# Moving a normalization step by one slot, widening a PSUM-slot rule, shifting two weight chunks, and transposing a row through HBM in a two-layer transformer kernel

## The chip, the cores and the metric

The kernel runs on all 8 cores of one Trainium2 chip. Each core computes one of the 8 sequences of the batch on its own; no data goes between cores. The metric is the device time of the slowest core, in microseconds.

## What is computed

Two "sandwich" layers, `x = x + LN(f(LN(x)))` each time, on x of 2048 x 1024 per core:

```python
# layer 0: latent attention, causal, 16 heads, head size 64 + 32 rotary
scores = einsum('bhqd,bhkd->bhqk', Q, K); scores = clip(scores, -80, 80); causal mask
attn = softmax(scores / sqrt(96)) @ V ; out = attn @ W_O
# layer 0: FFN with 8-bit fixed-point inputs and weights, ReLU, 1024 -> 4096 -> 1024
# layer 1: plain attention, not causal, 16 heads of 64
# layer 1: FFN with ternary weights and RMS norm of both inputs
def _ternary_linear(x, w):
    alpha = mean(abs(w)); w_t = sign(w) * (abs(w) > 0.5 * alpha)
    rms = sqrt(sum(x * x, -1)) / sqrt(d)
    return einsum('bsd,fd->bsf', x / (rms + EPS), w_t)
h = gelu(_ternary_linear(x, w_up)); out = _ternary_linear(h, w_down)
```

## The kernel before

**The program.** Each engine has its own list of instructions, in the order in which the Python code calls `P.op` and `P.group`. Waits are worked out from named resources: a reader waits for the last writer, a writer for the last writer and all readers. An engine runs its list strictly in order, so a wait at its head holds all behind it, DMA issues too. DMAs are issued from SP (`sync`), from ACT (`scalar`) and from POOL (`gpsimd`). A DMA waits as its resources say, and also for the DMA four places earlier on its own queue.

**An attention head** (`emit_attention_head`, used by both layers). Keys are in 16 blocks of 128, queries in two halves of 1024. An item n is one key block against one half: `emit_scores` (two matmuls of 512 columns, L462), `emit_expmask` (one Exp on ACT from PSUM to `pbuf`, L481; in layer 0 also a clamp and a mask on DVE, L485 and L492) and `emit_pv` (two matmuls that accumulate into `psB`, L512). The causal layer has 8 items in the first half (n = 0 to 7) and 16 in the second (8 to 23), layer 1 has 16 and 16 (0 to 15, 16 to 31). After the items come "extras", projections for the next head (8 in layer 0; 4 in layer 1, in every second head). Step n of the loop emits: the exp of item n-1, the scores of item n, the PV of item n-2, then `norm_tick(n)`. `pbuf` has two slots, item n uses slot n % 2, so the exp of n waits for the PV of n-2.

The scores go to one of three PSUM slots, by `slot_of(n)`: `psA.s0`, `psA.s1`, and as third the half of `psB` that PV is not accumulating into (banks b0 and b1 while the second half runs). Just after the first half is done, b0 and b1 still hold its result, so the items in a window at the start of the second half are "unsafe" and take `n % 2` in `psA` instead of the third slot.

**Normalizing a head.** When the last PV of the first half is emitted, blocks 0 and 1 are queued. Each `norm_tick` first emits a due "s2", then an "s1" of the next queued block. s1 is a reciprocal of the 1 x 512 row of sums on DVE (L525) and a copy of the block to `scrA` (ACT L531 in layer 0, DVE L535 in layer 1). s2 is a matmul with one row that broadcasts the reciprocal back into the block's PSUM bank (L544) and a multiply on DVE that reads this bank (L551 in even heads, L557 in odd ones). For layer 1, s1(0) is emitted at n = 18, s1(1) at 19, s2(0) at 20, s2(1) at 21. For layer 0 the four are at n = 10, 11, 12 and 13. Blocks 2 and 3 follow likewise after the last item; where there are no extras they are emitted at the end, outside the loop.

**The mean of |w|** (`mk_alpha`). 128 chunks of the two ternary weights are loaded on ACT's queue (L1515) through a ring of two and summed by an ACT Abs (L1501). `chunk()` number i emits the Abs of chunk i-2, then the load of chunk i, so 130 calls do it all. 32 calls lie in the V projection of layer 1, 12 at the start of each of its 8 head pairs, and `emit_block_ffn1` emits what is left (two calls) before it uses the sums (L1552).

**The last FFN** (`emit_block_ffn1`, `emit_ffn_matmul_phase`). It runs over 4 groups of 512 tokens (jt). Each has an up phase (8 weight bands `w1b`, L1028, with a sum of squares by a ones-matmul into `ps_dn0`, L1647), then `down_pre`, then a down phase (16 weight chunks `w2b` in two buffers, L1051), then the closing layer norm. In jt = 0 the weights come in f32 from SP and POOL (L975, L1004), are quantized on DVE (L1083, L1086) and stored from ACT; in jt = 1 to 3 the quantized bands and chunks are loaded from POOL (L964, L993). `down_pre` turns the 512 sums of squares, one row, into a factor per token (scale L1664, square root on ACT L1667, add L1669, reciprocal L1672) and turns the row into four columns of `rstd2T`. The columns are used only as `scale` in the closing layer norm (L368), after the whole down phase. The POOL DMAs of chunks 0 and 1 are emitted behind `down_pre`.

Of the kernel before, what the change touches and what calls it, by code (L numbers as in the profile page):

```python
# [10 lines left out]
F32 = mybir.dt.float32  # L11
# [414 lines left out]
def emit_attention_head(P, h, qk_lhsT, qk_rhs, qk_res, v_km, attn, psA, psB,  # L426
# [4 lines left out]
    half_last = {}  # L431
# [7 lines left out]
    N = len(items)  # L439
# [3 lines left out]
    def slot_of(n):  # L443
        s = n % 3
        half = items[n][1] if n < N else 1
        unsafe = (n < N and half == 1 and n < half_last[0] + 7)
        if s == 2 and unsafe:
            s = n % 2
        if s < 2:
            return psA, s * 1024, (f"psA.s{s}",)  # L450
        w = (1 - half) * 1024
        return psB, w, (f"psB.b{2 * (1 - half)}", f"psB.b{2 * (1 - half) + 1}")
# [86 lines left out]
    def emit_norm_s2(b):  # L539
        bres = f"psB.b{b}"  # L540
        rr = rrow[b % 2]
        scr = scrA[b % 2]
        sres = f"scrA{b % 2}"
        P.op("tensor", lambda e, b=b, rr=rr: e.matmul(  # L544
            psB[0:64, b * 512:(b + 1) * 512], P.consts["ones_f"][0:1, 0:64],
            rr[:], start=True, stop=True),
            reads=(f"rrow{b % 2}", "c_ones_f", sres), writes=(bres,))
        col0 = (h // 2) * S + b * 512
        if not odd:
            P.op("vector", lambda e, scr=scr, col0=col0, b=b:  # L550
                 e.tensor_tensor(attn[0:64, col0:col0 + 512],  # L551
                                 scr[:], psB[0:64, b * 512:(b + 1) * 512],
                                 ALU.mult),
                 reads=(sres, bres), writes=("attn",))
        else:
            P.op("vector", lambda e, scr=scr, b=b:
                 e.tensor_tensor(astage[:, b * 512:(b + 1) * 512],  # L557
                                 scr[:], psB[0:64, b * 512:(b + 1) * 512],
                                 ALU.mult),
                 reads=(sres, bres), writes=("astage",))  # L560

    norm_s1q = []
    norm_s2q = []

    def norm_tick(n):
        if norm_s2q and norm_s2q[0][0] <= n:
            emit_norm_s2(norm_s2q.pop(0)[1])
        if norm_s1q:
            b = norm_s1q.pop(0)
            emit_norm_s1(b)  # L570
            norm_s2q.append((n + 2, b))

    for n in range(M + 2):
        if 1 <= n < M + 1:
# [23 lines left out]
    if odd:  # L598
        col0 = (h // 2) * S
        P.op("gpsimd", lambda e, col0=col0: e.dma_start(  # L600
            out=attn[64:128, col0:col0 + S], in_=astage[:]),
            reads=("astage",), writes=("attn",), dma=True)
# [636 lines left out]
def emit_block_l1(P, hw):  # L1239
# [8 lines left out]
        writes=("v_km.ones",))  # L1248
# [19 lines left out]
    else:  # L1268
# [20 lines left out]
        out=vwT[:].rearrange("p (k m) -> p k m", m=D),  # L1289
        in_=vwt_h.rearrange("(k p) m -> p k m", p=128)),  # L1290
        writes=("vwT",), dma=True)
    for kc in range(NT):
        fns = []
        for dc in range(NCH):
            for n2 in range(2):
# [4 lines left out]
                    start=(dc == 0), stop=(dc == 7)))  # L1300
# [6 lines left out]
            reads=("psA.s0", "v_km.ones", "VBC"), writes=("v_km",))  # L1307
# [114 lines left out]
    for j in range(8):  # L1422
        bs = j % 2
        qpair, kpair = qpair_b[bs], kpair_b[bs]
        qpr, kpr = f"qpair{bs}", f"kpair{bs}"
        if "alpha" in hw:
            for _ in range(12):
                hw["alpha"]["chunk"]()
        if j + 1 < 8:
            pair_loads(j + 1)  # L1430
        for hh in range(2):
            h = 2 * j + hh
            base = hh * 64

            def qk_lhsT(kc, base=base, kpair=kpair):
                return kpair[base:base + 64, kc * 128:(kc + 1) * 128]

            def qk_rhs(lo, width, base=base, qpair=qpair):
                return qpair[base:base + 64, lo:lo + width]

            extra = pair_prod_items(j + 1) if (hh == 0 and j + 1 < 8) else ()
            emit_attention_head(
                P, h, qk_lhsT, qk_rhs, (qpr, kpr), v_km, attn,
                psA, psB, pbuf, causal=False, exp_scale=1.0,
                exp_bias=negb[bs][:], exp_bias_res=f"negb{bs}",
                clamp=None, mask0=None, scrA=scrA, rrow=rrow, astage=astage,
                extra_items=extra, evac_eng="vector")
            if hh == 0 and j + 1 < 8:
                pair_bounds(j + 1)
# [8 lines left out]
        out=owT[:].rearrange("p (k m) -> p k m", m=D),  # L1458
        in_=owt_h.rearrange("(k p) m -> p k m", p=128)),
        writes=("owT",), dma=True)  # L1460
# [5 lines left out]
    for i in range(NT):  # L1466
        half = i % 2
        pres = f"psA.s{half}"
        fns = []
        for c in range(NCH):  # L1470
            for n2 in range(2):
# [4 lines left out]
                    start=(c == 0), stop=(c == 7)))  # L1476
# [55 lines left out]
def emit_block_ffn1(P, hw):  # L1532
# [4 lines left out]
                                kind="Internal").ap()  # L1537
    wdnq_hbm = P.nc.dram_tensor("wdnq_scr", [DFF, D], BF16,
                                kind="Internal").ap()

    al = hw["alpha"]
    while al["idx"][0] < 130:
# [48 lines left out]
    else:  # L1591
# [6 lines left out]
         reads=("lnd.var",), writes=("lnd.sv",))  # L1598
    P.op("vector", lambda e: e.tensor_tensor(
        sv[:], sv[:], stats["rstd"][:], ALU.mult),  # L1600
        reads=("lnd.sv", "lnd.rstd"), writes=("lnd.rms",))
    P.op("vector", lambda e: e.tensor_scalar(
        sv[:], sv[:], float(EPS_RMS), None, ALU.add),
        reads=("lnd.rms",), writes=("lnd.d2",))
    P.op("vector", lambda e: e.reciprocal(scl[:], sv[:]),
         reads=("lnd.d2",), writes=("lnd.f",))
    P.op("vector", lambda e: e.tensor_tensor(
        scl[:], stats["rstd"][:], scl[:], ALU.mult),
        reads=("lnd.f", "lnd.rstd"), writes=("lnd.scl",))
    P.op("vector", lambda e: e.tensor_tensor(  # L1610
        nms[:], stats["mean"][:], scl[:], ALU.mult),
        reads=("lnd.scl", "lnd.mean"), writes=("lnd.nms",))
    P.op("vector", lambda e: e.tensor_scalar(
        nms[:], nms[:], -1.0, None, ALU.mult),
        reads=("lnd.nms",), writes=("lnd.nms",))
# [16 lines left out]
    r2row = P.sb("r2row", [1, 512], F32, st_mm)  # L1632
    rstd2T = P.sb("rstd2T", [128, 4], F32, st_mm)
# [7 lines left out]
    phase = {}  # L1641
# [19 lines left out]
    def down_pre(jt, _ps=[None]):  # L1661
        rms_mm(31)
        ps_dn0 = phase["ps_dn0"]
        P.op("vector", lambda e: e.tensor_scalar(  # L1664
            r2row[:], ps_dn0[:, 0:512][0:1, :], float(1.0 / DFF), None,
            ALU.mult), reads=("ps_dn0",), writes=("r2row",))
        P.op("scalar", lambda e: e.activation(  # L1667
            r2row[:], r2row[:], AF.Sqrt), reads=("r2row",), writes=("r2row",))
        P.op("vector", lambda e: e.tensor_scalar(  # L1669
            r2row[:], r2row[:], float(EPS_RMS), None, ALU.add),  # L1670
            reads=("r2row",), writes=("r2row",))
        P.op("vector", lambda e: e.reciprocal(r2row[:], r2row[:]),  # L1672
             reads=("r2row",), writes=("r2row",))
        for qc in range(4):
            P.op("tensor", lambda e, qc=qc: e.matmul(
                phase["ps_dn1"][:, 0:1], r2row[0:1, qc * 128:(qc + 1) * 128],
                P.consts["ones_f"][0:1, 0:1], start=True, stop=True),
                reads=("r2row", "c_ones_f"), writes=("ps_dn1",))
            P.op("vector", lambda e, qc=qc: e.tensor_copy(
                rstd2T[:, qc:qc + 1], phase["ps_dn1"][:, 0:1]),  # L1680
                reads=("ps_dn1",), writes=("rstd2T",))
        return lambda qc: (rstd2T[:, qc:qc + 1], "rstd2T")

    emit_ffn_matmul_phase(P, xnT, "xnT", hbuf, wupq_hbm, wdnq_hbm, st_mm,
# [109 lines left out]
```

How the kernel before makes its waits and increments, by code:

```python
        def run(e, f=f, waits=tuple(waits), sem=sem, incv=incv):  # L127
            for sn, v in waits:
                e.wait_ge(sems[sn][0], v)
            f(e).then_inc(sems[sem][0], incv)
# [12 lines left out]
        def run(e, fns=tuple(fns), waits=tuple(waits), sem=sem):  # L143
            for sn, v in waits:
                e.wait_ge(sems[sn][0], v)
            for f in fns[:-1]:
                f(e)
            fns[-1](e).then_inc(sems[sem][0], 1)
# [9 lines left out]
        def run(e, wl=wl):  # L158
            for sn, v in wl:
                e.wait_ge(sems[sn][0], v)
```

## Time and profile before

| | us |
|---|---|
| median of 2 runs | 4989.59 (4989.36 to 4989.81) |
| the profiled execution | 4985.35 |
| its span on the slowest core (core 5) | 4983.8 |
| spans of the other cores | 4924.1 to 4971.8 |
| PE busy | 3458.0 (69%) |
| DVE busy | 1753.5 (35%) |
| ACT busy | 1706.9 (34%) |
| POOL busy | 193.8 (4%) |
| chain that ended last, by engine | PE 49%, DVE 16%, DMA 15%, ACT 10%, issue 9% |

On core 5 the attention of layer 0 runs from about 240 to 1170 us, the first FFN to about 2160, the attention block of layer 1 to about 4062 (its heads from about 2374 to 3897), the last FFN to the end; its groups of tokens begin their down phases at 4230, 4447, about 4650 and 4860 us. The profile gives for each engine its instructions with start and duration, and for an idle engine what ended the wait. "PEclk" is the granted clock of TensorE as a share of full speed: 0.50 is 1.2 GHz, 1.00 is 2.4 GHz. The time of the profiled execution is 1.6 us more than the span of its slowest core.

### The profile page before, as it was taken

How to read it: one execution, taken by the hardware profiler on the slowest of the kernel's cores; microseconds unless marked ns; L12 is line 12 of the kernel's file. 1: busy time of each engine (PE TensorE's matmuls, PEld its weight loads, DVE VectorE, ACT ScalarE, POOL GpSimd, SP SyncE). 2: the span in 40 equal slices, each digit the busy share in tenths (PEclk: the TensorE clock that was granted, in tenths of full speed). 3: DMA queues.
4: the chain of work that ended last, by engine and by line, in shares of the span. 5: the costliest groups of instructions: out<-in, count | busy, mean ns of one | idle time of the engine just before them, and what ended most of it. 6: DMA issues, size and time to landing. Idle time of an engine off the chain costs nothing.

```text
span 4983.8 us, 49101 instructions; the slowest of 8 cores (4924.1 to 4983.8 us)
## 1 busy us (share of the span) xinstructions
PE 3458.0 (69%) x10539; PEld 1026.2 (21%) x10539; DVE 1753.5 (35%) x2312; ACT 1706.9 (34%) x2110; POOL 193.8 (4%) x272
## 2 busy tenths in 40 slices
PE   2577777775436668745888788878879647687785
PEld 1122222221112223322111111111111122222222
DVE  4355555555632432332222313222232563401111
ACT  3044455442233311231444353443434233123130
POOL 0000000000000011100000000000000000000100
PEclk9666666666668889968555555555555668899977
DMA  3000000001047424322010110110100107622213
GB/s 84 14 5 5 5 5 5 6 5 20 1 127 224 131 86 126 102 61 67 9 32 1 32 32 1 32 32 0 32 26 2 19 17 212 201 77 93 93 59 127
DMA packets 132278, 275.25 MB, mean 55 GB/s; under 512 B 25731, under 2 KB 60979, under 8 KB 132022
## 3 DMA queue, kind: packets, MB, share of 16 engines
q0 software_dynamic: 62208, 154.22, 11.4%
q10 hardware_dynamic: 45840, 75.51, 4.5%
q1 hardware_dynamic: 23974, 42.38, 2.8%
q8 instruction: 127, 2.08, 0.2%
q14 instruction: 129, 1.06, 0.1%
HBM read 237.02 MB, written 41.94 MB: 56 GB/s over the span
## 4 chain that ended last, share of the span: by engine, by line
PE 49%; DVE 16%; DMA 15%; ACT 10%; issue 9%; DVEq 1%; ACTq 1%; POOLq 0%; SPq 0%; POOL 0%
PE psB L512 12%; PE psA L462 9%; PE ps_up L1028 8%; ACT pbuf L481 4%; PE ps_dn L1051 3%; PE psB L462 3%; PE psB L544 3%; PE ps_dn L1647 2%; DVE rrow L525 2%; DMA w2b<-w2q_scr 2%; DMA w2q_scr<-w2b 2%; DMA wdnq_scr<-w2b 2%; DMA al_wf<-wdnt 2%; DMA w2b<-wdnq_scr 2%; DVE xs L409 1%
## 5 line engine op out<-in xcount | busy, mean ns | idle before, releaser
L512 PE MATMUL psB<-pbuf,v_km 128*65 128x512 bf16 (+3 forms) x1664 | 798.4, 572 | 198.3 <-ACT pbuf L481 115.1
L525 DVE RECIPROCAL rrow<-psB 1x512 f32<-1x512 f32 x128 | 426.5, 3341 | 864.0 <-PE psB L512 861.7
L481 ACT ACTIVATE pbuf<-psA,negb 128x1024 bf16<-128x1024 f32 x384 | 426.0, 1114 | 400.0 <-PE psB L512 380.0
L1051 PE MATMUL ps_dn<-w2b,hbuf 128*128 128x512 bf16 x1536 | 404.6, 403 | 124.0 <-ACT w2b L1075 33.2
L462 PE MATMUL psA<-qpair,kpair 64*128 64x512 bf16 x768 | 392.4, 617 | 29.7 <-ACT pbuf L481 26.0
L1028 PE MATMUL ps_up<-xqT,w1b 128*128 128x512 bf16 x1024 | 247.9, 405 | 171.5 <-DVE hscr L1187 91.6
L481 ACT ACTIVATE pbuf<-psA,nb 128x1024 bf16<-128x1024 f32 (+7 forms) x288 | 255.4, 894 | 274.1 <-PE psB L512 152.8
L512 PEld LDWEIGHTS psB<-pbuf,v_km 128*65 128x65 bf16 x1664 | 175.5, 143 | 779.1 <-issue 772.7
L462 PE MATMUL psA<-qh,kh 96*128 96x512 bf16 (+3 forms) x496 | 213.7, 523 | 135.2 <-DMA qh<-qraw 79.6
L1028 PE MATMUL ps_up<-xnT,w1b 128*128 128x512 bf16 x1024 | 258.8, 399 | 25.6 <-DVE w1b L1086 19.0
L544 PE MATMUL psB<-rrow,c_ones_f 1*64 1x512 f32 x256 | 211.8, 921 | 93.0 <-DVE scrA L535 77.9
L485 DVE TENSOR_SCALAR pbuf<-pbuf 128x1024 bf16<-128x1024 bf16 (+7 forms) x384 | 131.2, 342 | 344.7 <-ACT pbuf L481 338.7
L1051 PEld LDWEIGHTS ps_dn<-w2b,hbuf 128*128 128x128 bf16 x1536 | 149.3, 102 | 349.0 <-issue 238.6
L1647 PE MATMUL ps_dn<-sqd,c_ones_cf 128*1 128x512 f32 x256 | 139.8, 629 | 70.5 <-ACT sqd L1657 70.5
L481 ACT ACTIVATE pbuf<-psB,negb 128x1024 bf16<-128x1024 f32 x128 | 142.6, 1114 | 104.1 <-PE psB L512 104.1
L317 PE MATMUL tp_pt<-s_identB,tp_ln 128*128 128x128 bf16 x512 | 64.7, 306 | 163.2 <-ACT tp_ln L297 95.9
L1028 PEld LDWEIGHTS ps_up<-xqT,w1b 128*128 128x128 bf16 x1024 | 103.6, 103 | 315.7 <-issue 214.3
L1187 DVE TENSOR_SCALAR hscr<-ps_up,B 128x512 int8<-128x512 f32 x128 | 95.8, 751 | 188.3 <-PE ps_up L1028 188.3
L1051 PE MATMUL ps_up<-w2b,hbuf 128*128 128x512 bf16 x512 | 161.2, 398 | 0.0
L1190 ACT ACTIVATE hbuf<-hscr 128x512 bf16<-128x512 int8 x128 | 80.6, 629 | 189.1 <-DVE hscr L1187 184.0
L1637 ACT ACTIVATE hbuf<-ps_up 128x512 bf16<-128x512 f32 x128 | 76.3, 596 | 199.7 <-PE ps_up L1028 194.6
L1028 PEld LDWEIGHTS ps_up<-xnT,w1b 128*128 128x128 bf16 x1024 | 93.1, 101 | 241.5 <-issue 173.3
(258 smaller groups left out, 3402.5 us busy)
## 6 DMA issues: line engine op xcount, KB each, us to landing
w1b<-w1q_scr POOLq DMA_DIRECT2D x24, 1024.0 KB, 6.2
w2b<-w2q_scr POOLq DMA_DIRECT2D x48, 512.0 KB, 3.9
w1b<-wupq_scr POOLq DMA_DIRECT2D x24, 1024.0 KB, 5.9
w2b<-wdnq_scr POOLq DMA_DIRECT2D x48, 512.0 KB, 3.9
al_wf<-wupt ACTq DMA_DIRECT2D x64, 256.0 KB, 2.9
al_wf<-wdnt ACTq DMA_DIRECT2D x64, 256.0 KB, 3.0
xs<-x SPq DMA_DIRECT2D x1, 8192.0 KB
wqf<-w1t SPq DMA_DIRECT2D x8, 1024.0 KB
```

Of the source, the lines that this page charges most:

```text
L462: fns.append(lambda e, kc=kc, lo=lo, nn=nn, gq=gq, pst=pst: e.matmul(pst[:, lo:lo + nn], qk_lhsT(kc), qk_rhs(gq, nn), start=True, stop=True))
L481: P.op("scalar", lambda e, sc_ap=sc_ap, pb=pb, kw=kw: e.activation(pb, sc_ap, AF.Exp, **kw), reads=pres, sreads=sr, writes=(pbres,))
L485: P.op("vector", lambda e, pb=pb: e.tensor_scalar(pb, pb, clamp[1], clamp[0], ALU.min, ALU.max), reads=(pbres,), writes=(pbres,))
L512: q_start=q_start, lastkc=lastkc: e.matmul(psB[:, gq:gq + nn][0:65, :], v_km[:, kc * (H * 65) + h * 65: kc * (H * 65) + h * 65 + 65], pb[: ...
L525: P.op("vector", lambda e, b=b, rr=rr: e.reciprocal(rr[:], psB[64:65, b * 512:(b + 1) * 512]), reads=(bres,), writes=(f"rrow{b % 2}",))
L544: P.op("tensor", lambda e, b=b, rr=rr: e.matmul(psB[0:64, b * 512:(b + 1) * 512], P.consts["ones_f"][0:1, 0:64], rr[:], start=True, stop=T ...
L1028: e.matmul(ps_up[:, slot * 512:(slot + 1) * 512], w1band[bs][:, k * 512 + hx * 128: k * 512 + hx * 128 + 128], xT[:, k * S + jt * 512: k * ...
L1051: hx=hx, dnp=dnp: e.matmul(dnp[:, n2 * 512:(n2 + 1) * 512], hbuf[:, hc * 512 + qc * 128: hc * 512 + qc * 128 + 128], w2band[bs][:, hx * D ...
L1187: e.tensor_scalar(ii[:], psum_ap, 16.0, B16[:, hc:hc + 1], ALU.mult, ALU.add),
L1190: P.op("scalar", lambda e, ii=ii, hc=hc: e.activation(hbuf[:, hc * 512:(hc + 1) * 512], ii[:], AF.Relu, scale=1.0 / 16.0), reads=(ri,), wr ...
L1637: P.op("scalar", lambda e, psum_ap=psum_ap, hc=hc: e.activation(hbuf[:, hc * 512:(hc + 1) * 512], psum_ap, AF.Gelu), reads=(psum_res,), wr ...
L1647: P.op("tensor", lambda e, sq=sq, hc=hc, ps_dn0=ps_dn0: e.matmul(ps_dn0[:, 0:512][0:1, :], P.consts["ones_cf"][:], sq[:], start=(hc == 0), ...
```

## The change

It has four edits:

1. The unsafe window of `slot_of` is one item longer. Only items with n % 3 == 2 are touched by it: in layer 0 that is item 14, which goes from `psB` to `psA.s0`; in layer 1 item 22 comes into the window, whose n % 3 is 1, so no item moves.
2. s2 is emitted three steps after s1 in place of two: in layer 1 s2(0) at n = 21 and s2(1) at n = 22, in layer 0 at 13 and 14.
3. The last head pair of layer 1 calls `chunk()` 14 times in place of 12, so that nothing is left for `emit_block_ffn1`.
4. `down_pre` no longer turns the row by four one-row matmuls and copies. ACT writes it to HBM, and four DMAs from POOL read it back, one column of 128 values each.

```diff
@@ emit_attention_head, slot_of
-        unsafe = (n < N and half == 1 and n < half_last[0] + 7)
+        unsafe = (n < N and half == 1 and n < half_last[0] + 8)
@@ norm_tick
             emit_norm_s1(b)
-            norm_s2q.append((n + 2, b))
+            norm_s2q.append((n + 3, b))
@@ emit_block_l1
-            for _ in range(12):
+            for _ in range(12 if j < 7 else 14):
                 hw["alpha"]["chunk"]()
@@ emit_block_ffn1
+    r2_hbm = P.nc.dram_tensor("r2_scr", [512], F32, kind="Internal").ap()
@@ down_pre
         P.op("vector", lambda e: e.reciprocal(r2row[:], r2row[:]),
              reads=("r2row",), writes=("r2row",))
+
+        P.op("scalar", lambda e: e.dma_start(
+            out=r2_hbm.rearrange("(o c) -> o c", o=1), in_=r2row[:]),
+            reads=("r2row",), writes=("r2_scr",), dma=True)
         for qc in range(4):
-            P.op("tensor", lambda e, qc=qc: e.matmul(
-                phase["ps_dn1"][:, 0:1], r2row[0:1, qc * 128:(qc + 1) * 128],
-                P.consts["ones_f"][0:1, 0:1], start=True, stop=True),
-                reads=("r2row", "c_ones_f"), writes=("ps_dn1",))
-            P.op("vector", lambda e, qc=qc: e.tensor_copy(
-                rstd2T[:, qc:qc + 1], phase["ps_dn1"][:, 0:1]),
-                reads=("ps_dn1",), writes=("rstd2T",))
+            P.op("gpsimd", lambda e, qc=qc: e.dma_start(
+                out=rstd2T[:, qc:qc + 1],
+                in_=r2_hbm[qc * 128:(qc + 1) * 128].rearrange(
+                    "(p o) -> p o", o=1)),
+                reads=("r2_scr",), writes=("rstd2T",), dma=True)
```

## Rows read from the trace of the kernel before

**Rows 1.** Busy by stretch: length, PE, PEld, DVE, ACT, POOL; PEclk, DMA share, GB/s.
```profile
240.00:1170.00 930.00, 675.41 (x1828) 196.63 (x1828) 511.55 (x858) 449.43 (x539) 19.58 (x39) 0.64 0.02 5
...
2400.00:3920.00 1520.00, 1223.83 (x2657) 236.93 (x2656) 384.86 (x264) 632.40 (x687) 15.90 (x21) 0.54 0.09 20
```

**Rows 2.** Timeline, layer 1, first head: start, duration, engine, line, [idle before <-releaser].
```profile
2405.45 1.01 PE L462 MATMUL psA<-qpair,kpair 64*128 64x512 bf16 x2 [1.62 <-ACT pbuf L481]
...
2412.27 1.06 PE L512 MATMUL psB<-pbuf,v_km 128*65 128x512 bf16 x2
2413.26 1.97 PE L544 MATMUL psB<-rrow,c_ones_f 1*64 1x512 f32 x2
2413.49 1.11 ACT L481 ACTIVATE pbuf<-psA,negb 128x1024 bf16<-128x1024 f32 x1 [0.84 <-PE psB L512]
...
2415.16 1.03 PE L462 MATMUL psA<-qpair,kpair 64*128 64x512 bf16 x2
...
2420.97 1.03 PE L462 MATMUL psB<-qpair,kpair 64*128 64x512 bf16 x2
```

**Rows 3.** Timeline, layer 0, ninth head, start of its second half.
```profile
730.52 1.96 PE L544 MATMUL psB<-rrow,c_ones_f 1*64 1x512 f32 x2
...
732.35 0.35 DVE L485 TENSOR_SCALAR pbuf<-pbuf 128x1024 bf16<-128x1024 bf16 x1
...
733.25 1.06 PE L512 MATMUL psB<-pbuf,v_km 128*65 128x512 bf16 x2
...
737.20 1.01 PE L462 MATMUL psB<-qh,kh 96*128 96x512 bf16 x2 [1.00 <-DVE attn L551]
...
738.86 1.06 PE L462 MATMUL psA<-qh,kh 96*128 96x512 bf16 x2
```

**Rows 4.** PE's waits in the heads of layer 0: us in total, times, longest.
```profile
PE psB L462 <- DVE attn L551: 8.0, 8, 1.0
```

**Rows 5.** Busy time by stretch, same head, just after it.
```profile
738.00:741.00 3.00, 3.00 (x9) 1.12 (x8) 0.43 (x1) 1.19 (x2) 0.00 (x0) 0.50 0.00 0
741.00:745.00 4.00, 2.68 (x12) 0.89 (x10) 1.47 (x4) 3.16 (x3) 0.00 (x0) 0.95 0.02 6
```

**Rows 6.** Timeline, last FFN, around `down_pre` of jt = 3.
```profile
4821.51 1.41 POOL L993 DMA_DIRECT2D w2b<-wdnq_scr  x2
...
4850.02 0.68 DVE L1664 TENSOR_SCALAR r2row<-ps_dn 1x512 f32<-1x512 f32 x1 [105.28 <-PE ps_dn L1647]
...
4853.32 3.34 DVE L1672 RECIPROCAL r2row<-r2row 1x512 f32<-1x512 f32 x1
...
4860.39 2.74 PE L1051 MATMUL ps_dn<-w2b,hbuf 128*128 128x512 bf16 x6
```

**Rows 7.** Timeline, last FFN, around `down_pre` of jt = 0.
```profile
4219.76 3.34 DVE L1672 RECIPROCAL r2row<-r2row 1x512 f32<-1x512 f32 x1
...
4227.18 0.75 DVE L1083 TENSOR_SCALAR wqi<-wqf,ainv_bc 128x1024 int8<-128x1024 f32 x1
...
4230.35 2.72 PE L1051 MATMUL ps_dn<-w2b,hbuf 128*128 128x512 bf16 x6 [3.51 <-DVE w2b L1086]
```

**Rows 8.** Chain that ended last, layer 0: a POOL DMA behind a DVE result.
```profile
764.97 0.49 issue
765.47 1.86 DMA qh<-qraw
```

**Rows 9.** DMA issues: queue, count, KB each, us to landing (median).
```profile
w2b<-wdnq_scr POOLq DMA_DIRECT2D x48, 512.0 KB, 3.9
...
al_wf<-wdnt ACTq DMA_DIRECT2D x64, 256.0 KB, 3.0
```

**Rows 10.** Timeline: the last `chunk()` of pair 7; the two left over.
```profile
3736.70 0.33 ACTq L1515 DMA_DIRECT2D al_wf<-wdnt  x1
3737.24 2.12 ACT L481 ACTIVATE pbuf<-psA,negb 128x1024 bf16<-128x1024 f32 x2 [0.68 <-ACT al_wf L1501]
...
4062.49 0.63 ACT L1501 ACTIVATE al_wf<-al_wf 128x512 f32<-128x512 f32 x1 [2.65 <-issue]
```

## The prediction

> **What bounds the kernel now.** I read first the chain that ended last: TensorE (PE) has about half of it (the table of the profile above), and DVE and DMA a sixth each. No single engine bounds the whole, so each edit has to be read in its own stage. The busy times by stretch show what the stages are like [rows 1]. In the heads of layer 1, PE works 1224 of 1520 us, at a mean granted clock of 0.54, so at 1.2 GHz for most of the time; ACT works only 632 us. A wait that PE gains there is lost time. In the heads of layer 0, PE works 675 of 930 us, and PE, ACT and DVE wait for each other in turn.
>
> Then I read the timeline at the places that the edits touch. In layer 1 [rows 2] the reader is to see two things. Item 17 has the same score slot as item 16 (17 is unsafe and takes 17 % 2 = 1; 16 % 3 = 1), and its scores wait 1.62 us for the exp of 16. Items 20 and 21 also share a slot (20 % 2 = 0, 21 % 3 = 0), and yet the scores of 21 at 2415.16 do not wait: between the PV of 18 (2412.27) and them stands s2(0), 1.90 us of PE work from 2413.26, and the exp of 20 (2413.49 to 2414.60) runs beside it. The s2 matmul covers a slot conflict. In layer 0 [rows 3] the scores of item 14 go to `psB` right behind s2(1) and wait 1.00 us for the multiply that reads that bank. PE's wait list has it 8 times for L551, the even heads [rows 4], and in the same way 8 times for L557, the odd ones.
>
> **Edits 1 and 2 in layer 1.** No item changes its slot. s2(0) moves behind the PV of 19, s2(1) behind the PV of 20. The scores of 21 now follow the PV of 18 directly. They could start at 2413.26, but must wait for the exp of 20, which ends at 2414.60: at least 1.34 us, and by item 17, the same case without cover, 1.62 us. I take 1.62. Next, item 23 is the first to use `psB` (23 % 3 = 2, and the longer window still ends before 23). Before, one item (22) lay between s2(1) and it; now it follows s2(1) with nothing between on PE. That is the case of item 14 in layer 0 before, 1.00 us [rows 3]. Both waits are PE idling in a stretch where PE sets the pace, and nothing later in the head makes them up: 2.62 us x 16 heads = **+42 us**. The s2 of blocks 2 and 3 come out in the same order as before in layer 1 (they are at the end of the loop or behind it).
>
> **Edits 1 and 2 in layer 0.** Here item 14 goes to `psA.s0`, so the wait of 1.00 us is gone. But s2(0) now comes one step later, and with it goes a cover. The scores of 13 start at 730.52 in its place, and the PV of 11 could follow at about 731.4. It needs the clamp of 11, which stands on DVE behind the reciprocal of block 1 and runs from 732.35 to 732.70 [rows 3]. So this PV starts at about 732.85, only 0.40 us before its old time (733.25), with s2(0), 1.90 us, still to be done. Up to the scores of 15 the sum is 1.90 - 0.40 - 1.00 = +0.5 us; these were at 738.86 and come at about 739.4. They share `psA.s0` with item 14 now, but s2(1) stands between and covers the exp of 14. x 16 = +8 us. On top, the clock: it is at 0.50 until 741, some 4 us after a run of scores and PV begins at 737.20, and 0.95 in the stretch behind (1.2 and near 2.4 GHz) [rows 5]. With the s2 matmul moved back, that run begins with item 15 in place of 14. If the rise follows its beginning, one item more (1.7 us of PE work, two pairs of matmuls of about 0.85) is done at 1.2 GHz; as ACT needs 1.1 us for an exp anyway, that costs about 0.5 us, x 16 = +8. The bounds are 0 and 8 for this; I take 8, since PE was also busy before 737.20, with an s2 matmul among its work, and the rise came only with the items after it. Together **+16 us**. At the end of a layer 0 head the s2 of blocks 2 and 3 also move, but there DVE is the chain and does the same operations before the last rotary step; I cost that at nothing, and its cover is DVE's own queue.
>
> **Edit 3.** The two added calls at pair 7 each sum a chunk that is still on its way. The last load is issued at 3736.70 and takes 3.0 us [rows 9, 10]; with its Abs (0.63 and 0.2 for reading the sum) and the 0.68 us before the first exp, the exp starts at about 3741.2 in place of 3737.24 [rows 10]. PE is waiting for it: +4.0 us. At the start of the last FFN the two Abs from 4062.49 are gone, 0.63 + 0.2 us each, -1.6 us. Sum **+2 us** (bounds 0 and 4).
>
> **Edit 4.** What it takes away: PE had to stand still until the reciprocal was done and four small matmuls had gone back and forth with DVE. In jt = 3 the row of sums is read by 4850.70 (4850.02 + 0.68), and the first down matmul starts at 4860.39 [rows 6]. With the edit PE has nothing to do with the reciprocal. What it adds is in POOL's queue. The loads of chunks 0 and 1 were issued at 4821.51, 29 us before they were needed [rows 6]. They are emitted behind `down_pre`, and POOL runs in order. With the edit, four DMAs stand in front of them. The first waits for the write of the row to HBM, which waits for the reciprocal (end 4856.66). And all four write the one resource `rstd2T`, so each waits until the one before has landed. The chunks, long prefetched until now, are late next, and PE waits for them.
>
> The trace has no DMA of 2 KB behind a compute result. The nearest is one of 64 KB on POOL: 0.49 us of issue and 1.86 us to landing, 2.35 in all [rows 8]. The write and three reads must land before the fourth read is issued: 4 x 2.35 = 9.4, then 0.49 and about 0.5 for the fourth's issue, gives 4867.1; the load of chunk 0 needs 3.9 us [rows 9] and about 0.4 to release PE: 4871.4 against 4860.39, +11.0 us. Chunk 1 is 0.7 us behind it and has chunk 0's matmuls as cover. That is jt = 1, 2 and 3: +33. In jt = 0 the second half of chunk 0 is POOL's. The reciprocal ends at 4223.10 [rows 7]; + 9.4 + 1.0 + 3.9 = 4237.4, and its two DVE operations take about 1.6 us (two halves take 3.17, from 4227.18 to 4230.35 [rows 7]): PE starts at 4239.0 in place of 4230.35, +9. Together **+42 us**. Bounds: a round of 1.9 us would give +35 in all; landing in 3.0 us, as a 256 KB load on ACT's queue [rows 9], 3.5 a round, gives +60.
>
> **Sum.** 42 + 16 + 2 + 42 = +102 us. Against the profiled execution's own 4985.35 us that is 5087; its time is 4.2 us under the median of the runs, and on the median, 4989.6, the prediction is **5092 us**, 2.0% slower.
>
> **Rivals.**
> *A: the transfers are hidden (5015 us).* `rstd2T` is needed only some 80 us later, and PE is freed. The down phases would start right behind 4850.70, 9.6 us earlier x 3, and jt = 0 by 4.1 us (its DVE work could follow 4223.10 in place of 4227.18): -33. With the attention terms: +27. For it speaks how late the value is used; against it that the same queue carries the chunks. This is what the Trainium skill, "DMA: Bandwidth & Descriptors", section "Rules for kernel authors", advises: issue a DMA early, compute, and wait for it late. By that rule the time would be that of this rival.
> *B: the cover in layer 1 is not needed (5065 us).* If the scores of 21 are not held, a head of layer 1 pays only 1.00 us: 16 + 16 + 2 + 42 = +76. Against it speaks the wait of item 17.
> *C: small DMAs are slow (5115 us).* 3.5 us or more per round, +60 for edit 4, +120 to 125 in all. For it speaks that the reads scatter 4 bytes to each of 128 partitions, which no row shows.
> *D: faster (about 4800 us).* The s2 matmuls use one row of the array. If their place decided whether the clock rises in layer 1 as it does in layer 0 [rows 5], an item would fall from some 2.0 us (1.01 and 1.06 for its two pairs [rows 2]) to perhaps 1.3; it decides from the point where the clock rises by the first quarter of a second half. 12 items x 0.65 x 16 heads = -125, and in both halves about twice as much, against +60 from the rest. Against it: the 20 or so items of a head that have no s2 near them are also slow, since the stretch's mean is 0.54 at 80% busy [rows 1]. The Trainium skill, "TensorE: Matmul & The Clock Gate", section "Part 1: The HAM clock gate", says that activity releases the throttle. By busy time alone this trace does not agree in layer 1.
> *E: edits 1 and 2 do nothing in layer 0* (5076 us), if the freed wait and the lost cover cancel; it lies in the main range.
>
> **How the numbers follow.** Forecast with E: 76%, own range 5070 to 5108. A 8%, B 7%, C 6%, D 3%. The range 5064 to 5116 takes in B and C and leaves out A and D and the ends. A measurement of this kernel tells about 2% from no change, and that bound is 5089: the forecast lies on it. Of the forecast's 76%, 44 are above and 32 below; with C 50% slower by over 2%, with A and B 47% within 2%, with D 3% faster.
>
> **What would show it.** In layer 1, one new wait of PE for the exp at L462, so 32 in place of 16, and 16 waits of `psB` scores for the multiplies L551 and L557; in layer 0 these 16 gone, and a wait at L512 for L485 instead. In the last FFN, L993 DMAs issued some 10 us behind the reciprocal, and the first down matmul waiting for `w2b`. Before the first exp of head 14, PE waits about 4 us longer. I would be wrong if the chunk loads are issued before the row is back, if small DMAs land in other than about 2 us, or if the clock in either attention changes.

## The result

The changed kernel takes 5093.62 us (median of 11 runs) against 4977.34 us for the kernel before (10 runs): a ratio of 1.0215, 95% interval 1.0185 to 1.0244, so slower by some 107 us. The two medians lie 116 us apart; the ratio leaves out executions in which the chip's granted clock was lower, such as one of the 11. The interval contains 2%, so it stays open whether the loss is over 2%. The profiled execution took 5085.73 us, the one of before 4985.35.

To see where the time went, I cut each trace of all 8 cores at three events that every version has: the first load of `w_ob` (in layer 0's attention), the load of `VBC_row` (start of layer 1's V projection) and that of `OBC_row` (behind layer 1's heads). These are the means over the 8 cores, in us; all the tables below use them, and between versions that do the same in a stage they differ by up to some 4 us.

| | layer 0 attention | first FFN | layer 1 heads | last FFN, with what leads to it |
|---|---|---|---|---|
| before | 1168.6 | 1040.1 | 1687.9 | 1060.0 |
| after | 1178.6 | 1037.5 | 1732.8 | 1109.8 |
| difference | +10.0 | -2.6 | +44.9 | +49.8 |
| predicted | +16 | 0 | +42 and +4 of edit 3 | +42 and -2 of edit 3 |

**What TensorE waits for after.** PE's waits over the whole span of the changed kernel: what it waited for, then us in total, times, longest.

```profile
PE psA L462 <- ACT pbuf L481: 104.7, 65, 1.8
PE ps_dn L1051 <- DMA w2b<-wdnq_scr: 102.8, 25, 23.5
...
PE ps_dn L1051 <- DVE w2b L1086: 46.7, 10, 25.9
...
PE psB L512 <- DVE pbuf L485: 23.8, 16, 2.0
...
PE psB L462 <- DVE attn L551: 8.0, 8, 1.0
PE psB L462 <- DVE astage L557: 8.0, 8, 1.0
```

The first row was 78.0 us in 48 waits before, the second 29.8 us with a longest of 3.3, the third 28.4 with a longest of 5.9, the fourth 6.3 us in 13. The last two rows have the numbers of [rows 4], but their 16 waits now lie in layer 1 and no longer in layer 0.

**Layer 1, first head**, timeline of the changed kernel (start, duration, engine, line, [idle before <-releaser]), which answers to [rows 2]:

```profile
2422.16 1.12 ACT L481 ACTIVATE pbuf<-psA,negb 128x1024 bf16<-128x1024 f32 x1 [0.84 <-PE psB L512]
2423.63 1.01 PE L462 MATMUL psA<-qpair,kpair 64*128 64x512 bf16 x2 [1.62 <-ACT pbuf L481]
...
2425.57 1.97 PE L544 MATMUL psB<-rrow,c_ones_f 1*64 1x512 f32 x2
...
2429.42 1.96 PE L544 MATMUL psB<-rrow,c_ones_f 1*64 1x512 f32 x2
...
2431.55 0.68 DVE L551 TENSOR_TENSOR attn<-scrA,psB 64x512 bf16<-64x512 bf16 x1 [3.17 <-PE psB L544]
2432.38 1.01 PE L462 MATMUL psB<-qpair,kpair 64*128 64x512 bf16 x2 [1.00 <-DVE attn L551]
```

The reader is to see both new waits: 1.62 us of the scores of item 21 (2423.63) for the exp of item 20, and 1.00 us of the scores of item 23 (2432.38) for the multiply behind the s2 matmul at 2429.42.

**Last FFN, jt = 3**, timeline of the changed kernel, which answers to [rows 6] (from L1540 on, a line number is one higher than before up to the reciprocal, which is L1673):

```profile
4942.09 3.34 DVE L1673 RECIPROCAL r2row<-r2row 1x512 f32<-1x512 f32 x1
4945.56 0.22 ACTq L1676 DMA_DIRECT2D r_scr<-r2row  x1
4947.40 0.56 POOL L1680 DMA_DIRECT2D rstd2T<-r_scr  x1 [32.41 <-DMA r_scr<-r2row]
4950.29 0.55 POOL L1680 DMA_DIRECT2D rstd2T<-r_scr  x1 [2.33 <-DMA rstd2T<-r_scr]
4953.18 0.54 POOL L1680 DMA_DIRECT2D rstd2T<-r_scr  x1 [2.34 <-DMA rstd2T<-r_scr]
4956.34 0.54 POOL L1680 DMA_DIRECT2D rstd2T<-r_scr  x1 [2.63 <-DMA rstd2T<-r_scr]
4957.02 1.43 POOL L993 DMA_DIRECT2D w2b<-wdnq_scr  x2
4961.42 1.01 PE L1051 MATMUL ps_dn<-w2b,hbuf 128*128 128x512 bf16 x2 [22.81 <-DMA w2b<-wdnq_scr]
```

Each read is issued when the one before has landed, the loads of chunks 0 and 1 (L993) come behind all four, and PE stands idle for 22.81 us. From the end of the reciprocal (4945.43) to the first down matmul it is 15.99 us; before it was 3.73 [rows 6]. The profile's DMA table (KB each, us to landing) has for the reads:

```profile
w2b<-wdnq_scr POOLq DMA_DIRECT2D x48, 512.0 KB, 3.9
...
rstd2T<-r_scr POOLq DMA_DIRECT2D x16, 0.5 KB, 2.3
```

### The profile page after: what moved, and what is told of

The parts are those of the page before. It is cut to its first block, busy times and chain, and to the rows that moved or that the text cites. A ratio compares the mean times of both kernels' runs of the same rounds, so it can differ in the third digit from the quotient of the medians.

```text
span 5084.1 us, 49059 instructions; the slowest of 8 cores (5031.8 to 5084.1 us)
## 1 busy us (share of the span) xinstructions
PE 3451.7 (68%) x10507; PEld 1018.9 (20%) x10507; DVE 1749.2 (34%) x2296; ACT 1711.0 (34%) x2110; POOL 202.4 (4%) x288
## 4 chain that ended last, share of the span: by engine, by line
PE 50%; DMA 15%; DVE 14%; issue 10%; ACT 10%; DVEq 1%; ACTq 0%; POOLq 0%; SPq 0%; POOL 0%
PE psB L512 12%; PE psA L462 9%; PE ps_up L1028 9%; ACT pbuf L481 4%; PE ps_dn L1051 3%; PE psB L544 3%; PE ps_dn L1648 2%; PE psB L462 2%; DMA w2b<-wdnq_scr 2%; DMA al_wf<-wdnt 2%; DMA w2b<-w2q_scr 2%; DMA wdnq_scr<-w2b 2%; DMA w2q_scr<-w2b 2%; PE psA L773 1%; DVE rrow L525 1%
## 5 line engine op out<-in xcount | busy, mean ns | idle before, releaser
L481 ACT ACTIVATE pbuf<-psA,nb 128x1024 bf16<-128x1024 f32 (+7 forms) x304 | 273.8, 908 | 343.6 <-PE psB L512 220.3
L462 PE MATMUL psA<-qh,kh 96*128 96x512 bf16 (+1 forms) x528 | 228.2, 525 | 147.1 <-DMA qh<-qraw 89.8
L1028 PE MATMUL ps_up<-xnT,w1b 128*128 128x512 bf16 x1024 | 255.2, 395 | 23.7 <-DVE w1b L1086 18.9
L485 DVE TENSOR_SCALAR pbuf<-pbuf 128x1024 bf16<-128x1024 bf16 (+7 forms) x384 | 129.7, 341 | 312.1 <-ACT pbuf L481 307.1
L462 PE MATMUL psB<-qpair,kpair 64*128 64x512 bf16 x256 | 131.9, 617 | 16.0 <-DVE attn L551 8.0
L1501 ACT ACTIVATE al_wf<-al_wf 128x512 f32<-128x512 f32 x128 | 80.7, 631 | 180.7 <-DMA al_wf<-wupt 95.0
```

The costliest lines, as they stand in the source:

```text
L462: fns.append(lambda e, kc=kc, lo=lo, nn=nn, gq=gq, pst=pst: e.matmul(pst[:, lo:lo + nn], qk_lhsT(kc), qk_rhs(gq, nn), start=True, stop=True))
L481: P.op("scalar", lambda e, sc_ap=sc_ap, pb=pb, kw=kw: e.activation(pb, sc_ap, AF.Exp, **kw), reads=pres, sreads=sr, writes=(pbres,))
L485: P.op("vector", lambda e, pb=pb: e.tensor_scalar(pb, pb, clamp[1], clamp[0], ALU.min, ALU.max), reads=(pbres,), writes=(pbres,))
L1028: e.matmul(ps_up[:, slot * 512:(slot + 1) * 512], w1band[bs][:, k * 512 + hx * 128: k * 512 + hx * 128 + 128], xT[:, k * S + jt * 512: k * ...
L1501: P.op("scalar", lambda e, f=f, i=i: e.activation(f[:], f[:], AF.Abs, accum_out=A[:, i:i + 1]), reads=(rf, "alphaA"), writes=(rf, "alphaA"))
```

## The experiments

### Each part alone

Three kernels split the change. The first is the kernel before with edit 4 alone:

```diff
+ r2row -> HBM (scalar queue); for qc in range(4): HBM -> rstd2T[:, qc] (gpsimd queue)
- for qc in range(4): matmul r2row slice -> ps_dn1; copy -> rstd2T[:, qc]
```

> The kernel before with edit 4 alone. Theory (the four reads stand in POOL's queue in front of the chunk loads): the first down matmul comes 12 to 13 us later than before in each of the four token groups, as in the changed kernel, and the whole is 42 to 50 us slower (+0.9%). Rival (the loss of the changed kernel is mostly in the attention, and the row through HBM is hidden): 0 to 33 us faster.

The second has edits 1 and 2 alone:

```diff
- unsafe = (... n < half_last[0] + 7)
+ unsafe = (... n < half_last[0] + 8)
- norm_s2q.append((n + 2, b))
+ norm_s2q.append((n + 3, b))
```

> The kernel before with edits 1 and 2 alone. Theory (lost covers): the heads of layer 1 end 42 us later relative to their start (16 x 2.62), those of layer 0 about 12 us later, the last FFN unchanged; together +54 us (+1.1%). Rival (the clock of layer 0 rises later because the s2 matmul lies later): +16 us or more in layer 0, and the rise comes 1.5 to 2 us later behind the scores of item 14 than before in most heads.

The third has edit 3 alone:

```diff
- for _ in range(12):
+ for _ in range(12 if j < 7 else 14):
```

> The kernel before with edit 3 alone. Theory: PE waits about 3 us longer at the start of head 14 (its wait was 9.0 us before and 11.8 us in the changed kernel), and the start of the last FFN is 1.5 to 2 us shorter; together within 2 us of the kernel before. Rival (the two sums left over cost nothing where they stood, since ACT is idle there): +3 us.

| | time, us (its own runs of before: 4975.37) | ratio (95%) | layer 0 | layer 1 heads | last FFN |
|---|---|---|---|---|---|
| edit 4 | 5026.38 | 1.0098 (1.0071 to 1.0124) | 1168.7 | 1687.1 | 1108.6 |
| edits 1 and 2 | 5033.39 | 1.0123 (1.0084 to 1.0162) | 1177.4 | 1730.0 | 1060.2 |
| edit 3 | 4972.51 (one run) | | 1168.7 | 1689.0 | 1059.8 |

The parts add up. Edit 4 makes the last FFN 48.6 us longer and touches nothing else. Edits 1 and 2 give +8.8 in layer 0, where I had expected about 12 and the rival 16 or more, and +42.1 in layer 1. Edit 3 moves layer 1 by +1.1 and the last stage by -0.2, which is no more than the scatter between versions: nothing to be measured. The sum, 48.6 + 8.8 + 42.1 + about 1 = 100, is the +102 of the changed kernel's stages (10.0 - 2.6 + 44.9 + 49.8) within that scatter.

### Which of edits 1 and 2

The kernel before with edit 1 alone:

```diff
- unsafe = (... n < half_last[0] + 7)
+ unsafe = (... n < half_last[0] + 8)
```

> Edit 1 alone: item 14 of layer 0 goes to psA.s0, s2 stays two steps behind s1. Theory (slots and cover): layer 1 unchanged, 1687 to 1689 us for its heads as before, since no item moves there. In layer 0 the wait of 1.00 us for the multiply before item 14 goes, and item 15, which has psA.s0 too and no s2 matmul between, waits up to 1.62 us for the exp of 14: heads of layer 0 from -1.0 to +0.6 us each, -16 to +10 us in all, so the +42 of layer 1 and most of the +9 of layer 0 come from edit 2. Rival (edit 1 carries the loss of layer 0): layer 0 longer by 9 us or more here.

It took 4990.46 us against 4972.21, ratio 1.0045 (1.0024 to 1.0065). Layer 1 is unchanged (1686.8), so its +42 is all edit 2's. But layer 0 took 1185.1, +16.5 us, more than with edits 1 and 2 together (+8.8). My bound of +10 was too low, and the rival, that edit 1 carries the loss of layer 0, was right. PE's waits on core 5 for this kernel, whole span:

```profile
PE psA L462 <- ACT pbuf L481: 104.3, 64, 1.9
```

The waits for the exp rise from 48 to 64 here too, now in layer 0: item 15 waits for item 14, which has the same slot, and the two rows for the 1.00 us waits are gone. That is 1.62 - 1.00 = 0.62 a head, 10 us. The other 6.5 us, 0.4 a head, are not a wait. They go with the clock. The traces show it between the scores of item 11 and those of item 17, which stand around both s2 matmuls in every version. In the mean over the 16 heads of all 8 cores this stretch takes 14.26 us before and 15.33 with edit 1. PE stands idle in it for 1.39 us before and 1.99 with edit 1, and works for 12.87 and 13.34 us, on the same matmuls. Of this work 1.71 us were done at the high clock (2.4 GHz) before, 1.32 with edit 1. So about 0.6 us a head is the longer wait and 0.5 the lower clock. With edit 2 added, s2(1) stands between items 14 and 15 and covers the exp, and 8 us come back.

### Is it the shared slot?

The changed kernel, all four edits, with one more rule for the window at the start of the second half: neighbours take the two `psA` slots in turn.

```diff
- if s == 2 and unsafe:
-     s = n % 2
+ if unsafe:
+     s = (n - half_last[0] - 1 + (1 - half_last[0] % 3 % 2)) % 2
```

> The changed kernel with all four edits, and the items of the unsafe window take the two slots of psA in turn, so that no two neighbours share one. Theory (the +45 of layer 1 are waits for a shared slot): items 17 and 21 of layer 1 no longer wait 1.62 us each for an exp; the 1.00 us of item 23 stays: heads of layer 1 shorter by 2 x 1.62 x 16 = 52 us than in the changed kernel, about 1681 in place of 1732.8. In layer 0 items 9 and 11 no longer share a slot with 8 and 10: 0 to -52 us, as there other waits may take their place. In all 5040 down to 4990 against 5094. Rival (the time comes from where the s2 matmuls stand, whatever the slots): layer 1 shorter by less than 26 us.

5015.54 us, ratio to before 1.0080 (1.0063 to 1.0098). Layer 1's heads took 1677.8 us, 55.0 less than in the changed kernel (1732.8), where 52 was expected. Two waits per head of 1.62 us, removed by nothing but the choice of slot, are thus worth what the wait list says, and the s2 matmuls stand where the change put them. Items of layer 1 in this kernel, core 5, from its timeline:

```profile
2398.77 1.03 PE L462 MATMUL psA<-qpair,kpair 64*128 64x512 bf16 x2
2400.73 1.96 PE L544 MATMUL psB<-rrow,c_ones_f 1*64 1x512 f32 x2
2403.69 1.01 PE L462 MATMUL psB<-qpair,kpair 64*128 64x512 bf16 x2 [1.00 <-DVE attn L551]
2405.62 1.03 PE L462 MATMUL psA<-qpair,kpair 64*128 64x512 bf16 x2
2407.58 1.03 PE L462 MATMUL psA<-qpair,kpair 64*128 64x512 bf16 x2
```

Only the 1.00 us of item 23 is left, and an item takes 1.96 us from start to start, which is the four matmuls of an item at 1.2 GHz and no wait. In layer 0 the turn-taking removes two waits of 1.62 a head as well (52 us in all), but gives only 11.3 us (1178.6 to 1167.3). PE's waits on core 5 show where a part of the rest went:

```profile
PE psB L512 <- DVE pbuf L485: 36.0, 32, 2.5
...
PE psA L462 <- ACT pbuf L481: 10.4, 16, 0.7
```

The PV matmuls wait 36.0 us for the clamp (L485), 12 more than in the changed kernel, and the exp still costs 10.4. Together that is 22 of the 41 us that are missing. The rest is a lower clock. Busy time in layer 0 on core 5, up to the load of `w_ob`, in the changed kernel and then in this one (length, PE, PEld, DVE, ACT, POOL; PEclk, DMA share, GB/s):

```profile
240.00:1179.10 939.10, 679.95 (x1828) 196.00 (x1828) 509.44 (x858) 450.28 (x539) 19.50 (x39) 0.65 0.02 5
...
240.00:1167.40 927.40, 709.93 (x1828) 201.15 (x1828) 509.54 (x858) 449.00 (x539) 19.09 (x38) 0.62 0.02 5
```

The same 1828 matmuls take longer: in the mean over the 8 cores PE is busy for 684 us in the changed kernel and for 708 here, 24 us more (the two parts come to 46 us, somewhat more than the 41). Between the scores of items 11 and 17 PE works 1.29 us a head at the high clock in the changed kernel and 0.10 here. Why the clock stays low there was not tested. So in layer 0 a wait removed came back partly as other waits and partly as a lower clock; in layer 1 PE sets the pace at 1.2 GHz with either order, and a wait removed is time gained.

### Is it the place in POOL's queue?

Four kernels take edit 4 alone and change only which queue has the four reads, when they are emitted, or what they wait for. First, the same reads from SP's queue:

```diff
- P.op("gpsimd", ... rstd2T[:, qc] <- HBM)
+ P.op("sync", ... rstd2T[:, qc] <- HBM)
```

> Edit 4 alone, with the four reads issued from SP in place of POOL, so that nothing stands in front of the chunk loads in POOL's queue. Theory (it is the queue order alone): the down phases of groups 1 to 3 start right behind the DVE read of the sums, 9.6 us earlier than before, group 0 some 4 us earlier; 28 to 33 us faster than before, 75 us faster than edit 4 on POOL. Rival (the row through HBM or the longer idle time itself is what costs): as slow as edit 4 on POOL, +40 us. Second rival (SP's own queue is needed in group 0): group 0 later than before, groups 1 to 3 earlier, in all 0 to 20 us faster.

4953.33 us, ratio 0.9955 (0.9939 to 0.9972); the last FFN took 1041.0, 19.0 us less than before and 67.6 less than with the reads on POOL. That is 14 us short of what the theory gave, and the timeline of jt = 0 on core 5 says why:

```profile
4221.24 0.45 ACTq L1676 DMA_DIRECT2D r_scr<-r2row  x1
4222.56 7.84 SPq L1680 DMA_DIRECT2D rstd2T<-r_scr  x4
4230.60 7.09 SPq L1004 DMA_DIRECT2D wqf<-wdnt  x3
...
4238.18 1.44 PE L1051 MATMUL ps_dn<-w2b,hbuf 128*128 128x512 bf16 x3 [23.82 <-DVE w2b L1086]
```

In jt = 0, and only there, SP loads half of each raw chunk, and these loads now stand behind the reads. The first down matmul comes 17.1 us behind the reciprocal in place of 7.25 [rows 7]: +9.8 us. In the other three groups it comes 1.00 us behind the last sum of squares in place of 10.55, -9.55 each. 9.8 - 28.7 = -18.9: the whole of the -19.0.

Second, the reads stay on POOL ahead of the chunks, but write four resources, so that they do not wait for each other:

```diff
- writes=("rstd2T",)
+ writes=(f"rstd2T.{qc}",)
  # the closing norm reads rstd2T.{qc} likewise
```

> Edit 4 alone, but the four reads write four resources, so that they do not wait for each other; they are still issued from POOL before the chunk loads. Theory (a chain of dependent DMAs ahead of the chunks in one in-order queue): three rounds of 2.9 to 3.4 us go, and three issues of about 0.5 us stay: the last FFN 3 x 2.5 x 4 = 30 us shorter than with edit 4 alone, about 1079 in place of 1108.6 us, still 19 longer than before, as the chunks still stand behind the write. Rival (the reads share something, memory or the engine's descriptors, and take their time in any case): less than 10 us shorter.

4993.06 us, ratio 1.0040 (1.0029 to 1.0052); last FFN 1079.6, 29.0 less than edit 4 alone, as the theory had it (30), and still 19.6 over before. Timeline, jt = 2, core 5:

```profile
4647.41 0.24 ACTq L1676 DMA_DIRECT2D r_scr<-r2row  x1
4649.26 2.55 POOL L1680 DMA_DIRECT2D rstd2T<-r_scr  x4 [32.43 <-DMA r_scr<-r2row]
4652.41 1.43 POOL L993 DMA_DIRECT2D w2b<-wdnq_scr  x2 [0.60 <-DMA rstd2T<-r_scr]
4656.80 1.01 PE L1051 MATMUL ps_dn<-w2b,hbuf 128*128 128x512 bf16 x2 [16.34 <-DMA w2b<-wdnq_scr]
```

Four issues take 2.55 us together, where the chain of four in the changed kernel took 9.5 (4947.40 to 4956.88). The chunk load then waits 0.60 us more for the read four places ahead of it in its queue. So of the 48.6 us of edit 4, 29 are the reads waiting for each other, and the other 20 are the chunk loads behind the reciprocal, the write and the issues.

Third, the reads as in edit 4 (POOL, one behind the other), but emitted behind the down matmuls, just ahead of the closing layer norm:

```diff
  down_pre: row -> HBM as in edit 4
- for qc in range(4): gpsimd read of column qc
+ def cols(qc):            # called ahead of the closing norm, qc = 3 first
+     if qc == 3: the four gpsimd reads
+     return rstd2T[:, qc:qc + 1], "rstd2T"
```

> Edit 4 alone, the same five DMAs on the same queues and with the same resources, but the four reads are emitted behind the down matmuls, just ahead of the closing layer norm that uses them, so that the chunk loads stand ahead of them on POOL. Theory (only the place in POOL's queue costs): the chunks are prefetched as before, the down phase starts as soon as its row of sums is read, 9.6 us earlier in three groups and 4.1 us in the first: the last FFN 33 us shorter than before, about 1027 us, the kernel about 4942 against 4975. Rival (the small DMAs cost in themselves, or the reciprocal still holds what the down phase needs): 1050 us or more in the last FFN.

4950.07 us, ratio 0.9950 (0.9934 to 0.9967); last FFN 1037.5, 22.5 under before, between the two expectations. The start of the down phases is as the theory says: the first matmul 2.98 us behind the reciprocal in jt = 0 (before 7.25), and 1.00 us behind the sums in the other three (before 10.55); that is 4.3 + 3 x 9.55 = 32.9 us. Ten of them are given back. The timeline at the end of jt = 0, core 5:

```profile
4293.57 0.54 POOL L1682 DMA_DIRECT2D rstd2T<-r_scr  x1 [2.99 <-DMA rstd2T<-r_scr]
4294.31 1.78 POOL L964 DMA_DIRECT2D w1b<-wupq_scr  x2 [0.21 <-issue]
...
4302.48 4.00 PE L1028 MATMUL ps_up<-xnT,w1b 128*128 128x512 bf16 x9 [11.98 <-DMA w1b<-wupq_scr]
```

The next weight loads in POOL's queue, the up bands of jt = 1, are now the ones behind the reads. The first up matmuls wait 11.98 us, and before the idle time there was 1.6 to 3.3 us. The closing norm waits for the reads too: its L368 at 4297.07 is released by the DMA of `rstd2T`, where before PE released it. In the last group, with no up phase behind it, the time from the last down matmul to the end is 56.7 us in the mean over the cores, 5.3 more than with the reads from SP below. Most of the stall had moved to what stands behind the reads. The last run of this series tests that: the late reads, from SP.

```diff
- P.op("gpsimd", ... late reads)
+ P.op("sync", ... late reads)
```

> Edit 4 alone, the four reads emitted behind the down matmuls, as in the kernel with the late reads, but issued from SP, which in groups 1 to 3 issues nothing else. Theory (what the reads hold up is what stands behind them in their queue): neither the chunk loads nor the next group's first up band wait; the down phases start 9.6 us earlier in three groups and 4.3 us in the first, and the 10 us per group that the late reads on POOL gave back at the next group's first w1b stay: last FFN 33 us shorter than before, about 1027 us, against 1037.5 with the late reads on POOL. Rival (the 10 us come from the closing layer norm, which waits for the late reads, whichever queue has them): about 1037 us again.

4941.09 us, ratio 0.9933 (0.9909 to 0.9957); last FFN 1023.7, 36.3 under before, where 33 were expected; the 3 us between lie within the scatter of the stages. The same place in its timeline:

```profile
4290.82 3.17 SPq L1682 DMA_DIRECT2D rstd2T<-r_scr  x2
4299.08 1.11 ACT L368 ACTIVATE pod_o<-ps_up,rstd2T 128x1024 f32<-128x1024 f32 x1 [100.89 <-PE ps_up L1051]
...
4300.55 3.61 PE L1028 MATMUL ps_up<-xnT,w1b 128*128 128x512 bf16 x16 [1.57 <-ACT pod_o L368]
```

The closing norm (L368) waits for PE, not for a read, and the up phase follows it after 1.57 us. The same five DMAs, on the same bytes, cost 48.6 us in one place and gain 36.3 in another.

### Together

The kernel before with the two changes that gained: slots in turn, and late reads from SP, without edits 1 to 3.

```diff
+ s = (n - half_last[0] - 1 + (1 - half_last[0] % 3 % 2)) % 2   # in the unsafe window
+ row -> HBM in down_pre; four reads from "sync" ahead of the closing norm
```

> No edit 1 to 3. The kernel before, with late reads from SP for edit 4, and with the items of the unsafe window on the two slots of psA in turn. Theory: layer 1 loses the wait of item 17, 1.62 x 16 = 26 us, about 1662 against 1687.9; layer 0 loses about 11 us, as the turn-taking gave with all four edits, about 1157; the last FFN 33 us, about 1027: in all 70 us, about 4905 us against 4975. Rival for layer 1 (with the wait of item 17 gone, another takes its place, as s2(0) still comes at item 20 and the window is one item shorter): less than 10 us gained there.

4884.11 us against 4969.37, ratio 0.9827 (0.9804 to 0.9850): 85 us faster than the kernel before, some 209 us faster than the changed one. Layer 1's heads took 1660.3 (-27.6, where I had -26), the last FFN 1023.4 (-36.6), and layer 0 1147.2: -21.4, about twice what the same rule gave on top of edits 1 and 2. PE's waits on core 5, with the exp no longer first:

```profile
PE psB L512 <- DVE pbuf L485: 19.0, 28, 1.4
PE psA L462 <- ACT pbuf L481: 10.7, 17, 0.8
```

The waits of `psA` scores for an exp fall from 78.0 us to 10.7. The PV waits for the clamp are 19.0 us, against 36.0 in the kernel with all four edits and the turns, and PE is busy in layer 0 for 682 us in the mean over the cores, against 708 there (671 before). Both fit with the larger gain in layer 0; that it is the place of s2 which makes the difference was not tested by itself.

## Why the prediction was right

The forecast was 5092 us and +102; measured were 5093.62 and, by the stages, +102. That the times agree to 2 us is partly luck: I started from 4989.6 us, the median of two runs, and the kernel before has 4977.34 over ten, so the step between the medians is 116 us and by the ratio 107. The terms, one by one:

- **Layer 1, edits 1 and 2: +42 predicted, +42.1 measured with these edits alone.** Both waits are there with the lengths of the rows they were read from, 1.62 and 1.00 us. The step that carried this was to ask of each neighbouring pair of items which slot it takes and what stands between them on PE. Rival B (item 21 is not held) and rival D (the clock rises) are ruled out; PEclk of the heads of layer 1 stays 0.54 in the changed kernel.
- **Layer 0: +16 predicted, +10.0 measured.** The loss lies where I had looked: from the scores of item 11 to those of item 17 a head takes 14.26 us before and 14.90 after (mean over 16 heads of 8 cores), +0.64 a head or +10 in all. Rival E, nothing in layer 0, is ruled out. But the two halves of the term are not both what I had.

  The waits: PE is idle for 1.39 us of this stretch before and 1.50 after. The 1.00 us of item 14 is gone, and the wait of the PV for the clamp rises by 1.1 us, from 0.38 to 1.49, where I had 1.5. That is +0.1 a head in place of +0.5, +2 us in place of +8: I took all of the clamp's wait for new, and in the mean over the heads, though not in the ninth, a part of it was there before. Item 15, which shares item 14's slot and does not wait behind s2(1), is as described.

  The clock: on the same matmuls PE works for 12.87 us before and 13.40 after, +0.53 a head, +8.5 us, which is the size of my +8. The work done at the high clock falls from 1.71 to 1.29 us. The size came out, but I had read one stretch of one head.

  In the ninth head on core 5 the scores of item 15 come 11.84 us behind those of item 11 before (727.02 to 738.86) and 10.85 us after (733.24 to 744.09): 1.0 us less, where I had +0.5. In the mean over all heads it is 10.98 and 11.53, +0.55. The PV that waits 1.42 us for the clamp starts 2.33 us behind the scores of item 13, as predicted; what I did not foresee is a short rise of the clock there. Such an early rise, ahead of the scores of item 15, is in 73 of the 128 heads before and in 88 after, but [rows 5] are from a head that has none. Busy time by stretch, ninth head, changed kernel (length, PE, PEld, DVE, ACT, POOL; PEclk, DMA share, GB/s):

```profile
733.00:737.00 4.00, 3.76 (x9) 1.26 (x10) 4.00 (x3) 1.51 (x3) 0.00 (x0) 0.50 0.00 0
737.00:738.00 1.00, 0.64 (x2) 0.00 (x0) 1.00 (x1) 1.00 (x1) 0.00 (x0) 0.79 0.00 0
738.00:741.00 3.00, 1.94 (x6) 0.60 (x7) 1.49 (x4) 1.20 (x2) 0.00 (x0) 0.97 0.00 0
741.00:745.00 4.00, 4.00 (x8) 0.85 (x7) 1.44 (x4) 1.12 (x1) 0.00 (x0) 0.50 0.00 0
```

  and from its timeline, where the s2 pair takes 1.07 us and then 1.96:

```profile
739.06 0.59 PE L512 MATMUL psB<-pbuf,v_km 128*65 128x512 bf16 x2 [1.42 <-DVE pbuf L485]
739.58 1.07 PE L544 MATMUL psB<-rrow,c_ones_f 1*64 1x512 f32 x2
...
742.20 1.96 PE L544 MATMUL psB<-rrow,c_ones_f 1*64 1x512 f32 x2
```

  The moved s2 of blocks 2 and 3, costed at nothing, cost nothing: from the first projection matmul behind the items to the next head's scores it is 17.4 us before and 17.5 after on core 5, 17.5 and 17.4 on core 2.
- **Edit 3: +2 predicted (bounds 0 and 4), about +1 measured,** which is within the scatter. Before the first PV of head 14, PE waits 11.75 us in place of 9.05, +2.7 where I had +4.0: the last load was on its way for 2.7 us when its Abs began (issued at 3786.56, Abs at 3789.22), and the exp followed it at once. In the timeline of the changed kernel:

```profile
3786.56 0.33 ACTq L1515 DMA_DIRECT2D al_wf<-wdnt  x1
...
3789.22 0.63 ACT L1501 ACTIVATE al_wf<-al_wf 128x512 f32<-128x512 f32 x1 [1.09 <-DMA al_wf<-wdnt]
...
3789.85 2.10 ACT L481 ACTIVATE pbuf<-psA,negb 128x1024 bf16<-128x1024 f32 x2
```

- **Edit 4: +42 predicted, +49.8 measured (+48.6 alone).** The chain is as written: write, four reads one by one, then the chunk loads, then PE. The undersized term is the round. I took 2.35 us from a 64 KB DMA [rows 8]. From the starts of the reads (4947.40, 4950.29, 4953.18, 4956.34) a round is 2.9 to 3.2 us, 0.55 us of issue and 2.3 to 2.6 of landing. Behind the reciprocal the first down matmul came 11.9, 12.9, 12.6 and 12.3 us later than before in the four groups, 49.7 in all, against 9 + 3 x 11. That is inside the bounds I gave (35 to 60), towards rival C. Rival A, that the transfers hide, would have been right for this very edit with the reads behind the down matmuls and on another queue: then the last FFN is 36 us faster, near the -33 that I worked out for it. What the Trainium skill, "DMA: Bandwidth & Descriptors", section "Rules for kernel authors", advises (issue early, wait late) holds in that order of the work; in the changed kernel the reads were issued as early as they could be, and what was late was everything behind them in the queue.

The terms' errors, -6 in layer 0 (the waits), -1 in edit 3 and +8 in edit 4 (the round), cancelled; that the sum was nearer than its parts is luck.

Open: what the order of the work does to the clock. The traces say how much longer PE worked on the same matmuls, but a slower PE also waits less, and no run here held the clock while the order of the work changed.

## What to carry to other kernels

A DMA that waits for a late result holds every DMA issued behind it on its queue: before adding one, read what stands behind it there in every phase, also in the one that uses the queue differently, and emit it behind that or on a queue that has nothing left to do. A matmul that does something else can be the cover of a slot conflict between its neighbours; before moving it, go through the neighbours' slots, or let them take turns so that no cover is needed. Whether a wait removed is time gained depends on whether its engine sets the pace there, and on whether the clock stays what it was: 52 us of such waits gave 55 in layer 1 and 11 in layer 0, where they came back half as other waits and half as longer matmuls. And a rise or wait read from one head is checked against the mean over the heads before it is multiplied by 16.

## What was not expected of the hardware

A DMA of 0.5 KB that puts 4 bytes into each of 128 partitions landed in 2.3 us (median of 16), longer than the 1.86 us of the 64 KB one in [rows 8]; with its issue, a dependent round on POOL took 2.9 to 3.2 us. And PE can work without a gap and stay at 1.2 GHz. In layer 1, in the kernel with the turns (core 5, whose timeline is shown above), it worked for the whole of 2403.7 to 2420 us on score and PV matmuls, and the granted clock was 0.50 throughout:

```profile
2403.70:2420.00 16.30, 16.30 (x34) 2.64 (x34) 0.00 (x0) 8.23 (x8) 0.00 (x0) 0.50 0.00 0
```

In the ninth head of layer 0 it rose between 737 and 738 us behind 4 us in which PE had worked 3.76, and was at 0.50 again from 741 on, behind an idle time of 1.42 us.
